# Transposing the second batch's attention probabilities by VectorE and DMA instead of TensorE

## The reference

```
memory_proj    = memory @ W_mem.T                        # 2 x 1024 x 512, from memory 2 x 1024 x 256
scores         = hidden @ memory_proj.T / sqrt(512)      # 2 x 512 x 1024
attn           = softmax(scores)
memory_context = attn @ memory_proj                      # 2 x 512 x 512
gate  = sigmoid(concat(hidden, memory_context) @ W_gate.T + b_gate)
fused = hidden + gate * memory_context
out   = fused * rsqrt(mean(fused^2) + 1e-6) * norm_w
```

## Time and profile before

| | |
|---|---|
| Median of 3 runs | 125.65 us (125.37 to 125.92) |
| Profiled execution | 125.98 us |
| its span | 124.3 us |
| TensorE busy | 116.0 us (93%) |
| VectorE busy | 72.4 us (58%) |
| ScalarE busy | 55.0 us (44%) |
| GpSimd busy | 18.2 us (15%) |
| mean granted clock of TensorE | 0.987 |

### The profile page before, as it was taken

The page is one execution under the profiler, slowest core; times in us unless marked ns, Lnnn a source line. Parts: engine busy times, 40 slices in busy tenths (PEclk is TensorE's granted clock), DMA queues, the critical chain, the costliest instruction groups (busy, mean ns, idle before and its releaser), DMA issues.

```text
span 124.3 us, 1567 instructions
## 1 busy us (share of the span) xinstructions
PE 116.0 (93%) x561; PEld 96.3 (77%) x561; DVE 72.4 (58%) x111; ACT 55.0 (44%) x99; POOL 18.2 (15%) x25
## 2 busy tenths in 40 slices
PE   6799999999999999999999999999999999999900
PEld 6678788688888888888888888888888888888900
DVE  0397979887999401656856856856400012774791
ACT  4597576459887913735236226226000030233241
POOL 2000000000000698780100100100100000011030
PEclk9999999999999999999999999999999999999995
DMA  3999992237956750000220220320400000034204
GB/s 61 340 378 242 392 392 83 106 121 191 294 175 191 221 205 0 0 0 0 84 84 5 84 84 0 84 84 11 158 5 0 0 0 0 0 124 132 84 4 165
DMA packets 8215, 14.25 MB, mean 115 GB/s; under 512 B 912, under 2 KB 1680, under 8 KB 8208
## 3 DMA queue, kind: packets, MB, share of 16 engines
q1 hardware_dynamic: 7776, 13.50, 32.9%
q10 hardware_dynamic: 432, 0.66, 1.8%
HBM read 12.06 MB, written 2.10 MB: 114 GB/s over the span
## 4 chain that ended last, share of the span: by engine, by line
PE 87%; DMA 3%; DVE 3%; ACT 2%; issue 1%; POOLq 1%; POOL 1%; DVEq 0%; ACTq 0%
PE wide L605 18%; PE wide L671 18%; PE acc L655 18%; PE wide L683 9%; PE wide L698 8%; PE acc L580 7%; PE wide L619 6%; PE wide L633 4%; DMA ring<-xT 3%; DVE neg_max L413 1%; DVE probs L420 1%; ACT squares L335 1%; POOLq L29 1%; DVE gate L460 1%; DVE gate L453 1%
## 5 line engine op out<-in xcount | busy, mean ns | idle before, releaser
L437 DVE TENSOR_TENSOR wgT_lo<-acc,wgT_hi 128x512 fp32r<-128x512 f32 x4 | 2.6, 685 | 21.2 <-ACT wgT_hi L324 21.2
L303 ACT ACTIVATE probs<-wide,neg_max 128x1024 f32<-128x1024 f32 x8 | 8.9, 1116 | 11.6 <-DVE neg_max L413 11.6
L270 POOL TENSOR_TENSOR rstd<-mean_sq,neg_half 128x1 f32<-128x1 f32 x8 | 4.6, 574 | 61.2 <-ACT squares L335 60.1
L605 PE MATMUL wide<-ctxT_hi,qT_hi 128*128 128x512 f32 x32 | 12.9, 402 | 0.0
L605 PE MATMUL wide<-ctxT_hi,qT_lo 128*128 128x512 f32 x32 | 12.6, 394 | 0.0
L605 PE MATMUL wide<-ctxT_lo,qT_hi 128*128 128x512 f32 x32 | 12.5, 391 | 0.0
L328 ACT ACTIVATE gate<-gate 128x512 f32<-128x512 f32 x8 | 5.1, 632 | 16.1 <-DVE gate L447 16.1
L413 DVE TENSOR_REDUCE neg_max<-wide 128x1 f32<-128x1024 f32 x8 | 9.8, 1224 | 3.5 <-PE wide L605 3.3
L426 DVE TENSOR_TENSOR pT_lo<-wide,pT_hi 128x1024 fp32r<-128x1024 f32 x8 | 9.8, 1223 | 3.4 <-ACT pT_hi L312 3.4
L312 ACT ACTIVATE pT_hi<-wide 128x1024 fp32r<-128x1024 f32 x8 | 8.2, 1028 | 6.9 <-PE wide L619 6.9
L265 POOL TENSOR_TENSOR wgT_lo<-ring,wgT_hi 128x512 fp32r<-128x512 f32 x4 | 5.4, 1379 | 40.0 <-ACT wgT_hi L291 40.0
(11 more groups left out here) (86 smaller groups left out, 237.1 us busy)
## 6 DMA issues: line engine op xcount, KB each, us to landing
ring<-ctxT SPq DMA_DIRECT2D x8, 256.0 KB, 4.2
ring<-w_gateT SPq DMA_DIRECT2D x8, 256.0 KB, 4.6
ring<-ctxN SPq DMA_DIRECT2D x8, 256.0 KB, 4.5
xr<-x_rows SPq DMA_DIRECT2D x8, 256.0 KB, 2.7
out<-res SPq DMA_DIRECT2D x7, 256.0 KB, 2.0
ring<-xT SPq DMA_DIRECT2D x6, 256.0 KB, 5.8
ring<-w_mem SPq DMA_DIRECT2D x4, 128.0 KB, 4.6
ring<-xT ACTq DMA_DIRECT2D x2, 256.0 KB, 4.5
```

The lines of the kernel that those rows point to most:

```text
L303: nc.scalar.activation(probs[:, j % PROBS].rearrange("p (h m) -> p h m", h=2), wide[:, banks("scores", j)], ACT.Exp, bias=neg_max[:, j:j + 1],
L605: last = nc.tensor.matmul(wide[:, banks("scores", j), h], qT_s[left][:, c, rows], ctxT_s[right][:, c, cols], start=(c == 0 and (left, righ ...
```

## The change

In the second batch, `turn(4)` to `turn(7)` are gone. The probabilities of a tile are transposed in two steps. `square_up(t)` on VectorE transposes each square of 32x32 in its place and writes the result to two slots of `ring` (the slots in turn). The squares themselves must still change places across partitions: `send(t)` on SP writes the 512 KB to a DRAM tensor, and `fetch(t)` reads it back with four DMAs, one for each group of 32 partitions, in runs of 1 KB, into two further slots of `ring`. `placed_hi(t)` and `placed_lo(t)` then split it into `pT_s` as turned_hi and turned_lo did, with SBUF as their source.

The order on each engine is changed to match. TensorE does scores(5) directly after scores(4), and each later one a tile earlier than before. The ring of PSUM pairs has no turns in it for the second batch. ScalarE, VectorE and SP have their lists for this stretch written out anew. The eighth exponentials waits for square_up(0) instead of turn(4).

```
+        squares_of = [ring[:, 2 * n:2 * n + 2].rearrange("p a n -> p (a n)") for n in range(2)]
+        placed = [ring[:, 2 * n:2 * n + 2].rearrange("p a n -> p (a n)") for n in range(2, 4)]
+        passage = [nc.dram_tensor(f"passage{t}", [P, M], f32).ap() for t in range(T)]
...
-        for t in range(T):
-            uses += [("scores", T + t), ("gate", t), ("turn", T + t)]
-        uses += [("gate", T + t) for t in range(T)]
+        uses += [("scores", 4), ("scores", 5), ("gate", 0), ("scores", 6), ("gate", 1), ("scores", 7)]
+        uses += [("gate", j) for j in range(2, B * T)]
...
+            def next_x(j):
+                sp.wait_ge(fused, j - 1)
+                load_x(j)
...
+            def send(t):
+                sp.wait_ge(squared_up, t + 1)
+                sp.dma_start(passage[t], squares_of[t % 2]).then_inc(sent[t % 2], 16)
+            def fetch(t):
+                if t < 2:
+                    wait_lo(sp, NB - 1)
+                else:
+                    sp.wait_ge(pT_lo, T + t - 1)
+                sp.wait_ge(sent[t % 2], 16 * (t // 2 + 1))
+                quarters = passage[t].rearrange("(q j) (r f) -> r j q f", q=NQ, r=NQ)
+                for r in range(NQ):
+                    sp.dma_start(placed[t % 2][r * QUAD:(r + 1) * QUAD].rearrange("j (q f) -> j q f", q=NQ),
+                                 quarters[r]).then_inc(landed[t % 2], 16)
+            send(0)
+            fetch(0)
+            send(1)
+            fetch(1)
+            next_x(2)
+            store(0)
+            send(2)
+            fetch(2)
+            next_x(3)
+            store(1)
+            send(3)
+            fetch(3)
+            next_x(4)
+            store(2)
...
+            def placed_hi(t):
+                act.wait_ge(landed[t % 2], 16 * NQ * (t // 2 + 1))
+                if t == 0:
+                    act.wait_ge(a_sum, nth_chunk(0, KE - 1))
+                nc.scalar.activation(by_quarter(pT_s[0], t), from_quarters(t), ACT.Copy).then_inc(pT_hi, 1)
...
+            exponentials(4)
+            exponentials(5)
+            gate_tanh(0)
+            placed_hi(0)
+            mean_square(0)
+            exponentials(6)
+            gate_tanh(1)
+            placed_hi(1)
+            mean_square(1)
+            exponentials(7)
+            gate_tanh(2)
+            mean_square(2)
+            placed_hi(2)
+            gate_tanh(3)
+            placed_hi(3)
+            mean_square(3)
...
+            def square_up(t):
+                dve.wait_ge(normed, T + t + 1)
+                if t < 2:
+                    wait_lo(dve, NB - 7 + 2 * t)
+                    wait_hi(dve, NB - 7 + 2 * t)
+                else:
+                    dve.wait_ge(sent[t % 2], 16 * (t // 2))
+                nc.vector.transpose(squares_of[t % 2].rearrange("p (r k n) -> p k r n", r=NQ, k=KM),
+                                    probs[:, (T + t) % PROBS].rearrange("p (k r n) -> p k r n", r=NQ, k=KM))\
+                    .then_inc(squared_up, 1)
+            def placed_lo(t):
+                dve.wait_ge(pT_hi, T + t + 1)
+                nc.vector.tensor_tensor(by_quarter(pT_s[1], t), from_quarters(t),
+                                        by_quarter(pT_s[0], t).bitcast(f32), ALU.subtract).then_inc(pT_lo, 1)
...
+            row_max(4)
+            normalize(4)
+            row_max(5)
+            square_up(0)
+            normalize(5)
+            gate_arg(0)
+            square_up(1)
+            gated_context(0)
+            fuse(0)
+            row_max(6)
+            placed_lo(0)
+            finish(0)
+            normalize(6)
+            gate_arg(1)
+            square_up(2)
+            gated_context(1)
+            fuse(1)
+            row_max(7)
+            placed_lo(1)
+            finish(1)
+            normalize(7)
+            gate_arg(2)
+            square_up(3)
+            gated_context(2)
+            fuse(2)
+            placed_lo(2)
+            finish(2)
+            gate_arg(3)
+            gated_context(3)
+            fuse(3)
+            placed_lo(3)
+            finish(3)
...
             for t in range(T):
-                scores(T + t)
+                if t == 0:
+                    scores(4)
+                if t < T - 1:
+                    scores(5 + t)
                 gate_from_x(t)
                 gate_from_attended(t)
                 context(t)
-                turn(T + t)
```

More of the change, by code:

```diff
@@ L53, in xattn_kernel @@
         ring = sb("ring", [P, RING, BANK])
+        QUAD = 32
+        NQ = P // QUAD
+        squares_of = [ring[:, 2 * n:2 * n + 2].rearrange("p a n -> p (a n)") for n in range(2)]
+        placed = [ring[:, 2 * n:2 * n + 2].rearrange("p a n -> p (a n)") for n in range(2, 4)]
+        passage = [nc.dram_tensor(f"passage{t}", [P, M], f32).ap() for t in range(T)]
         probs = sb("probs", [P, PROBS, M])
@@ L159, in xattn_kernel @@
         ga_sum, mc_sum, mc_part = sem("ga_sum"), sem("mc_sum"), sem("mc_part")
-        turned = sem("turned")
+        turned, squared_up = sem("turned"), sem("squared_up")
+        sent = [sem(f"sent{n}") for n in range(2)]
+        landed = [sem(f"landed{n}") for n in range(2)]
         q_hi, q_lo = sem("q_hi"), sem("q_lo")
@@ L219, in wait_place, with by_quarter, from_quarters @@
                 eng.wait_ge(a_sum, nth_chunk(0, KE - 1))
+        def by_quarter(operand, t):
+            rows = operand[:, :, t * P:(t + 1) * P]
+            return rows.rearrange("p k (q n) -> p q k n", q=NQ)
+        def from_quarters(t):
+            return placed[t % 2].rearrange("p (q k n) -> p q k n", q=NQ, k=KM)
         block_ctx = ctx.enter_context(nc.Block())
@@ L239, in _, with store @@
                     load_x(1)
[L240 to L243, removed]
+            def next_x(j):
+                sp.wait_ge(fused, j - 1)
+                load_x(j)
+            def store(j):
                 sp.wait_ge(res_done, j + 1)
                 sp.dma_start(out[j], res[:, j % 2]).then_inc(stored[j % 2], 16)
+            def send(t):
[25 more added lines that the diff above has]
+            store(2)
+            for j in range(3, LAST):
+                if j + 2 < B * T:
+                    next_x(j + 2)
+                store(j)
             sp.wait_ge(last_left, 1)
@@ L300, in exponentials @@
                 act.wait_ge(maxed, j + 1)
-                if j >= PROBS:
+                if j - PROBS >= T:
+                    act.wait_ge(squared_up, j - PROBS - T + 1)
+                elif j >= PROBS:
                     act.wait_ge(turned, j - PROBS + 1)
@@ L305, in exponentials @@
                                      accum_out=row_sum[:, j:j + 1]).then_inc(exped, 1)
+            def placed_hi(t):
[3 more added lines that the diff above has]
+                nc.scalar.activation(by_quarter(pT_s[0], t), from_quarters(t), ACT.Copy).then_inc(pT_hi, 1)
             def turned_hi(j):
                 act.wait_ge(turned, j + 1)
-                if j == T:
-                    act.wait_ge(a_sum, nth_chunk(0, KE - 1))
                 rows = slice(j % T * P, (j % T + 1) * P)
```

## The result

The changed kernel takes 122.9 us (122.6, 122.87 and 122.92; a fourth execution took 124.86) against 125.65 before: 2.8 us less by the medians, 3.0 by the ratio of 0.976 (interval 0.973 to 0.979). Now and then an execution of either kernel takes 1.5% or more longer than the others, as that fourth one did; the times and ratios in this document leave such executions out, and a profile that was taken of one is given with its own time. On a second occasion the changed kernel had a median of 123.15 against 126.01, ratio 0.978 (0.975 to 0.980). The profiled execution took 122.92 us, for a span of 121.2.

The account below looks back on a forecast made before the run. TensorE was taken to bound the kernel. With the added work hidden, removing four turns starts attended(1) at 87.06 instead of 90.64, so 125.65 - 3.58 = 122.1 us; range 121.6 to 125.7, leaving out 2 in 10.

Parts of the forecast that it names:

- likeliest case: Second batch: the trip through DRAM is hidden behind TensorE's work, so attended(1) starts at 87.06; 121.7 to 122.6 us, chance 0.60.
- rival 2: Before attended(1): trip partly hidden, R between 7.2 and 8.5 or a transpose of 2 us or more; 122.7 to 125.0, chance 0.17.
- The chain and its ceiling: Second batch up to attended(1): TensorE runs back to back, so removing four turns gains at most 3.58 us.
- (a): square_up, one added VectorE transpose per tile, 128x1024 f32 in SBUF: 1.22 us, between 0.76 and 2.46.
- (b): send, 512 KB per tile from SBUF to DRAM: 2.7 us, between 2.0 and 4.0.
- (c): fetch, four 128 KB loads per tile into 32 partitions each: 2.7 + 1.0 = 3.7 us, between 3.4 and 5.9.
- (d): placed_hi and placed_lo, splitting each tile from SBUF in runs of 32: 1.03 and 1.23 us, at most double.
- R: Round trip from the end of square_up to landed data: 2.7 + 3.7 = 6.4 us, between 5.4 and 9.9.
- the trip is hidden: Before attended(1): pT_hi ready at 85.0 and pT_lo at 86.3, wanted at 87.06 and 87.5; slack 2.1 and 1.2 us.
- half rate into 32 partitions: Fetch: 32-partition loads move at half rate, movers 4.0 instead of 2.0 us, R 8.4; 124.8 us, chance 0.08.
- How it scales: Chain to attended(1): R is paid twice in series, free until 7.0, then 2 us for 1, break-even at 8.85.
- rival 4: At attended(1): R over 9.1, loads at quarter rate, TensorE idle 10.7 us, perhaps clock at 1.2 GHz; 132.8 us, chance 0.16.

Follow-up runs that it names:

- the run with the halves: The changed kernel with each send cut in two halves of 256 KB, the first two loads waiting for the first half only: 122.1 us, ratio 0.969.

## Why the prediction was right, and where it was off

- **Its own signs: two of them speak against it.** The prediction was to be wrong if the two DMAs together took over 7 us, and tile 7's took 7.4. It asked that TensorE have no idle time at the second `attended`, and there was a wait. placed_lo(3) was to end before 87.5 and ended at 87.58. The time, 122.9, lies outside the likeliest case's own 121.7 to 122.6 and inside rival 2's 122.7 to 125.0. The direction, the ceiling and most of the size are right by their mechanism. That the time lies in the stated range is owed to the range's width, which took in rival 2.
- **The chain and its ceiling: right.** TensorE sets the time, the four turns and what is lost around them are worth 3.58 us, and the new order alone is worth nothing. Without the trip the kernel takes the 122.1 us that were forecast.
- **(a) The transpose: right.** 1.23 us, taken as 1.22, and it stands three times in the chain. The Trainium skill ("Vector Engine (DVE) Microarchitecture Reference", the reshape front-end) has a transpose sustain one element per cycle per lane, and the trace agrees: 1.23 us, against the estimate of 1.07 us plus a start.
- **(b) The send: right alone, short in company.** 2.6 us for tiles 4 and 6, 2.7 forecast; 3.1 for tile 7 (3.4 in the second profile), with a load of x and a store issued 2.4 and 1.9 us ahead. I had checked that both are issued before the send, and not whether they still move while it does. With the store issued later, or 3.0 us ahead, the send took 2.6.
- **(c) The fetch: the mis-sized term.** 3.7 forecast, 4.2 measured. The fourth issue came 1.3 us after the first, as written, but the last load then took 2.8 to 2.9 of its own, longer than the 2.4 that the sum left it. I had added the movers' time to one landing; the issues stand in front of the last landing, and 1.3 + 2.9 is the sum.
- **(d) placed_hi and placed_lo: right**, 1.06 and 1.22, for 1.03 and 1.23. The runs of 32 cost 0.03 us at most.
- **So R was 6.85 and 7.4, not 6.4, and "the trip is hidden" is the step that failed.** pT_lo was complete at 87.6 instead of 86.3. TensorE wanted it at 87.0 instead of 87.5, since its first pair started at 86.53, in a stretch that had begun 0.31 earlier. The slack of 1.2 us became a wait of 0.6, or 0.8 until the products are back in step. That is the whole of the 122.9 against 122.1. The case that came true lies between forecast and rival 2: tile 7's R is in rival 2's 7.2 to 8.5, tile 4's is not, and neither half rate nor a slow transpose was behind it. (Rival 2's lower end is mis-summed as well: R = 7.2 gives 86.2 + 1.6 = 87.8, 0.3 late, which is 122.4 and not 122.7.)
- **Two terms that cancel.** The forecast's 86.2 with the two excesses, 0.45 and 1.0, gives 87.6 too, but in part by luck. square_up(0) ended 0.3 us earlier than forecast (57.98 against 58.3). And VectorE, which was to have no idle time behind placed_lo(0), waited 0.45 us for the norm's factor in front of finish(0) (the L551 line above). GpSimd makes that factor from mean_square(0), which stands behind placed_hi(0) on ScalarE. So tile 4's trip reaches VectorE by this way too, and it is this way that the chain takes. The prediction had it at nothing.
- **Rival 2's half rate into 32 partitions: refuted for these four loads.** The movers needed 0.3 us more per tile, not 2.0. Tile 7's 512 KB moved between 82.0 and 84.2 us at 240 GB/s, with a DMA share of 0.77: 1.7 us of the movers, where half the rate would have taken 4.0. The Trainium skill ("SBUF — State Buffer", Door 1) gives partitions 0 to 31 half of the ports, and no such limit shows here. But the four loads were in flight together, each landing 2.5 to 2.9 us after its issue and issued 0.44 us apart, and between them they write all 128 partitions. What one of them reaches by itself no run shows.
- **How it scales: only near the point where it was worked out.** "2 us for 1" held in the run with the halves (0.55 us less per trip, 1.1 in all), where tile 5's trip is hidden. With eight loads for four (10.3 us slower in all) it is paid too, the send of tile 7 is longer, and the clock comes on top.
- **The clock in rival 4: seen, and earlier than feared.** It fell without a 10 us wait: in one run 2.66 us idle, two products and 0.51 us idle came before the fall (1.6 us lost), while the 0.5 us of the changed kernel left it at 2.4 GHz (granted clock 1.00 from 84 to 96 us).

## What to carry to other kernels

A transfer in several DMAs is sized by the issues in front of its last one plus that one's own landing, with whatever else is moving at that time. The slack is compared with that, and not with the quiet case. Splitting the first of two transfers in series, so that the second starts on the first half, was worth more here than a better place for the store beside it. A wait or a DMA issue given to an engine with a list of its own moves to that engine's place in the list: look at what stands in front of it there.

## What the runs showed that was not expected

- A wait of TensorE can cost more than its length. After 2.66 and 0.51 us idle with two products between them, the granted clock was 0.50 for some 3 us, and 1.6 us were lost on top. After 8.55 us idle it was 0.50 as well, and 1.1 us were lost.
- A 512 KB load and a 512 KB store issued 0.4 us apart took 4.2 and 5.1 us. The same load with a 256 KB load of x 0.4 us behind it took 3.3, and the same store by itself 2.6.
- A 128 KB load into 32 partitions lands in 2.5 us when it is the first of four and 2.9 as the fourth. A 256 KB load into 128 partitions landed in 2.7 before.
